# Adding the mask to a quarter of the bias tiles on GpSimd, with stacks loaded in halves and a new table of slots

## Chip, cores and metric

The kernel runs on one core of a Trainium2 chip. The metric is device time in microseconds, the median over executions; a change below about 0.2% (2 us here) can't be told from none.

## What is computed

Sixteen sequences of 256 x 256 (float32) go through four layers. Layer 0 is a gradient and Laplacian step. Layer 1 is an adapter (down, gelu, a chosen expert, up, layer norm). Layer 2 is two modulated silu projections with norms over the whole matrix. Layer 3 is an attention block with 16 heads of 16 features and a feed-forward part of 1024. The change is in the attention:

```
scores = einsum('bhqd,bhkd->bhqk', q / sqrt(16), k)
scores = scores + attention_bias
scores = where(src_mask, -inf, scores)
probs = softmax(scores)
```

The bias is a tensor of 16 x 16 x 256 x 256; the mask is shared by the heads of a sequence. The kernel takes -1e30 for minus infinity and adds it.

## The kernel before

The work goes by **pairs** of sequences, eight of them, and a pair has 32 heads (16 for each sequence b = 0, 1). The function `run` writes out the order of every engine: a turn per pair has 32 **slots**, and slot n holds head n of pair j, steps of the `back` (what follows the attention) of the pairs j, j-1 and j-2, and steps of the `front` (layers 0 to 2 and q, k, v) of pair j+1 and the end of pair j's own. The table `AT` (with `AT_FIRST` for pair 0 and `AT_LAST` for the last) says in which slot each step of b = 0 and b = 1 stands; a slot of 32 or more is that slot less 32 of the next turn. Every engine walks the same slots in program order, at its own pace, and waits on semaphores. All 32 slots of pair 0's front come before the first head; after the last head only the back of the last pair is left.

A head goes through the engines like this:
- SyncE (`turn` at L462) loads the bias of heads in chunks of two into a ring of four buffers. A chunk waits until ScalarE is done with the chunk four before it (`prob_ok`). The same queue carries `load_stacks`, at positions given by `SP_AT`.
- TensorE (`scores`, L1321): a product of the identity with `mask_add` (bf16, 128 x 512, L1325) puts the mask of the head into PSUM; two products of the stacks (96 rows, bf16, L1328) add q times k. The stacks hold q and k split into bf16 parts; they are written to DRAM (L1006) and read back as six transfers for each sequence (L448).
- VectorE (`bias_and_max`, L893): L901 adds the PSUM scores and the bias tile and takes the row maximum, twice for each head.
- ScalarE: exp (L1038), and two heads later the copy of the turned probabilities (L1051). TensorE turns them (L1342) and multiplies four heads at once by V (L1363).

GpSimd runs what is left: two products of layer 0 (L554), additions of bias rows (L566, L575, L607), the scale and shift `x4` (L586, L588), the conversion of the mask (L536), and `inv_std` (L541), the power -1/2 that norms wait for. Those with 128 x 512 elements have eight forms (L554 has two), and each comes twice in a pair.

Steps that the prediction names: `hn` is the normalising of the attention output by VectorE (L646 with `ffT` as output), which waits for `inv5` on GpSimd; `ctx_spread` (L597) is a GpSimd copy that waits for the end of a group of heads on VectorE.

The four lines that put the mask in:

```python
pe.matmul(SP_[:, h % 2, :], identb[:, :], mask_add[:, 2 * b:2 * b + 2, :].rearrange("p q k -> p (q k)"),
          start=True, stop=False)
...
                    stacks[1][:, b, hh, :], start=False, stop=(q == 1))
```

Of the kernel before, what the change touches and what calls it, by code (L numbers as in the profile page):

```python
# [16 lines left out]
ALU = mybir.AluOpType  # L17
# [23 lines left out]
CH = 2  # L41
# [28 lines left out]
AT = {"x4": (21, 43), "ctx_spread": (16, 41), "ctx": (20, 36), "ctx_scale": (20, 36), "wo": (21, 37), "x5": (21, 38),  # L70
# [3 lines left out]
      "store": (46, 52), "prods_p": (1, 14), "prods": (1, 13), "diffs": (2, 15), "edges": (3, 15), "l0": (4, 17),  # L74
# [6 lines left out]
      "q_split": (25, 40), "q_out": (25, 42), "k": (25, 40), "kf": (25, 40), "k_split": (26, 41), "k_out": (26, 41),  # L81
      "v": (28, 45), "V": (29, 47), "mask": (20, 2)}
AT_FIRST = {"s_trig": (1, 1), "s_onehot": (2, 2), "s_grid": (1, 1), "s_h1": (1, 1), "s_h2": (5, 5), "s_h2t": (6, 6),
            "s_sel": (2, 2), "s_cond": (10, 10), "s_condt": (11, 11), "s_mask": (23, 23), "s_rows": (16, 16),
# [19 lines left out]
GROUPS = HEADS // GROUP  # L104
BATCHES = HEADS // BATCH


ORDER = [0, 2, 4, 6, 1, 3, 5, 7]
PR = 2
SIG = 1.702  # L110
WARM = {"begin": 50, ("w_in", 0): 8}


def wait_alone(eng, sem, value):


# [1341 lines left out]
```

## Time and profile before

| | |
|---|---|
| median of 3 runs | 993.87 us (991.92 to 994.06) |
| the profiled execution | 994.1 us, its span 992.3 us |
| TensorE matmul busy | 878.8 us, 89% of the span |
| VectorE busy | 767.2 us, 77% |
| ScalarE busy | 733.7 us, 74% |
| GpSimd busy | 238.5 us, 24% |
| first scores product | 102.1 us from the start |
| last head's scores | 958.5 us |

Six pairs in the middle repeat each other every 110.9 us. Busy time of TensorE is modelled: a matmul's record is longer than the distance to the next one (378 ns against 216 ns for 128 x 256 in float32), so the distance between starts is what one costs. Some records of L1325 are missing (168 of 256 matmuls, while the 256 weight loads are all there).

### The profile page before, as it was taken

The page shows a single profiled execution, that of the slowest core. Times are in us where ns is not written, and L with a number is a line of the kernel's source. Part 1 is how long each engine was busy: PE and PEld are TensorE (multiplying, and loading weights), DVE is VectorE, ACT ScalarE, POOL GpSimd, SP SyncE. Part 2 cuts the span into 40 slices and gives each one's busy share as a digit, 9 for nine tenths or more (in the row PEclk, how much of TensorE's full clock was granted, in tenths as well). Part 3 has the DMA queues.
Part 4 walks back from the last instruction along what each step waited for, and adds up shares of the span by engine and source line. Part 5 has one row for each costly group of instructions (what it writes and reads, how often), then busy time and mean ns, then how long its engine had stood idle before and what let it go on. Part 6 is the DMA issues. An engine that isn't in the chain of part 4 may idle for free.

```text
span 992.3 us, 17959 instructions
## 1 busy us (share of the span) xinstructions
PE 878.8 (89%) x5643; PEld 663.2 (67%) x5731; DVE 767.2 (77%) x2375; ACT 733.7 (74%) x1901; POOL 238.5 (24%) x237
## 2 busy tenths in 40 slices
PE   6775678998999989998999989998999989999988
PEld 5454455776777767776777767776777767766666
DVE  7366678978887988978887888888887988866532
ACT  2123578988788787978888787978789787978672
POOL 2124122312242222312242222312242223111100
PEclk8677789999999999999999999999999999999999
DMA  9714464463737364563628364553637273555500
GB/s 255 223 44 90 133 155 128 128 165 96 164 103 191 102 134 125 137 154 107 170 95 189 97 153 123 127 146 111 167 107 191 81 169 108 124 142 141 165 15 22
DMA packets 128472, 130.86 MB, mean 132 GB/s; under 512 B 16729, under 2 KB 121945, under 8 KB 125289
## 3 DMA queue, kind: packets, MB, share of 16 engines
q1 hardware_dynamic: 96464, 111.49, 43.5%
q10 hardware_dynamic: 31914, 18.23, 6.5%
q8 instruction: 46, 0.75, 0.3%
q14 instruction: 48, 0.39, 0.1%
HBM read 112.61 MB, written 17.07 MB: 131 GB/s over the span
## 4 chain that ended last, share of the span: by engine, by line
PE 54%; DVE 18%; ACT 16%; issue 7%; DMA 3%; POOL 1%; SPq 0%; DVEq 0%; ACTq 0%; POOLq 0%
PE ff_ps L1316 9%; PE PT_ps L1342 8%; PE ctx_ps L1363 5%; PE G L1112 5%; ACT Pr L1038 5%; PE scores_ps L1328 4%; PE ff_ps L1297 4%; DVE bias L901 3%; ACT L1038 3%; PE G L1197 3%; PE G L1120 3%; ACT PT L1051 2%; PE scores_ps L1325 2%; PE ff_ps L1283 2%; PE G L1193 2%
## 5 line engine op out<-in xcount | busy, mean ns | idle before, releaser
L1038 ACT ACTIVATE Pr<-bias,nmax 128x256 f32<-128x256 f32 x512 | 255.7, 502 | 135.2 <-DVE nmax L901 110.1
L901 DVE CUSTOM_DVE_ANT_0 bias<-scores_ps,bias 128x256 f32<-128x256 f32 x512 | 195.9, 420 | 85.8 <-issue 45.5
L1342 PE MATMUL PT_ps<-ident,Pr 128*128 128x128 f32 x1024 | 159.2, 278 | 9.4 <-ACT PT L1051 9.4
L1051 ACT ACTIVATE PT<-PT_ps 128x512 f32<-128x512 f32 x256 | 148.3, 579 | 0.2 <-PE PT_ps L1342 0.2
L1342 PEld LDWEIGHTS PT_ps<-ident,Pr 128*128 128x128 f32 x1024 | 117.3, 141 | 42.2 <-issue 27.1
L541 POOL TENSOR_TENSOR rstd<-var,half_neg 128x2 f32<-128x2 f32 (+1 forms) x64 | 40.4, 632 | 402.2 <-DVE var L666 233.3
L1297 PE MATMUL ff_ps<-ctxT,w 128*128 128x256 f32 x480 | 116.0, 384 | 7.1 <-ACT ffT L1025 6.3
L1316 PE MATMUL ff_ps<-w,ffT 128*128 128x256 f32 x480 | 112.3, 380 | 0.0
L1328 PE MATMUL scores_ps<-k_stack,q_stack 96*128 96x256 bf16 x512 | 99.9, 276 | 10.0 <-DMA k_stack<-part_dram 4.1
L1297 PEld LDWEIGHTS ff_ps<-ctxT,w 128*128 128x128 f32 x480 | 86.4, 190 | 20.6 <-ACT ffT L1025 10.3
L1038 ACT ACTIVATION_READ_ACCUMULATOR Pr<-bias,nmax 128x1 f32 x512 | 97.6, 191 | 0.0
L1316 PEld LDWEIGHTS ff_ps<-w,ffT 128*128 128x128 f32 x480 | 87.2, 190 | 10.2 <-issue 0.4
L1363 PE MATMUL ctx_ps<-PT,V 128*32 128x256 f32 x1024 | 68.8, 386 | 17.3 <-ACT PT L1051 17.3
L1328 PEld LDWEIGHTS scores_ps<-k_stack,q_stack 96*128 96x128 bf16 x512 | 51.0, 100 | 48.1 <-issue 2.5
L1325 PE MATMUL scores_ps<-mask_add,identb 128*128 128x512 bf16 x168 | 64.9, 387 | 1.1 <-issue 1.0
L1038 ACT ACT_TABLE_LOAD x44 | 56.5, 1283 | 5.4 <-DVE nmax L901 4.7
L880 DVE SCALAR_TENSOR_TENSOR ffT<-tanh,ffT 128x512 f32<-128x512 f32 x60 | 44.3, 738 | 18.7 <-ACT ffT L1025 18.7
L1363 PEld LDWEIGHTS ctx_ps<-PT,V 128*32 128x32 f32 x1024 | 28.0, 109 | 42.6 <-issue 20.5
L987 ACT ACT_TABLE_LOAD x31 | 39.8, 1283 | 17.5 <-DVE cond L743 13.5
L1021 ACT ACTIVATE tanh<-ff_ps,b1s 128x256 f32<-128x256 f32 x120 | 50.0, 471 | 3.0 <-PE ff_ps L1297 3.0
L1025 ACT ACTIVATE ffT<-ff_ps,b 128x256 f32<-128x256 f32 x120 | 50.8, 485 | 0.0
L597 POOL COPY tanh<-rinv 128x512 f32<-128x512 f32 x16 | 9.8, 610 | 146.9 <-DVE ctxU L913 146.9
(219 smaller groups left out, 1693.5 us busy)
## 6 DMA issues: line engine op xcount, KB each, us to landing
bias<-in_fside_Bx16xSxS_dram SPq DMA_DIRECT2D x256, 256.0 KB, 3.1
part_dram<-front ACTq DMA_DIRECT2D x32, 384.0 KB, 2.7
q_stack<-part_dram SPq DMA_DIRECT2D x16, 384.0 KB, 4.8
k_stack<-part_dram SPq DMA_DIRECT2D x16, 384.0 KB, 7.9
F<-in_x_dram SPq DMA_DIRECT2D x16, 256.0 KB, 3.8
ada<-rows_dram SPq DMA_DIRECT2D x16, 256.0 KB, 5.6
q_stack<-part_dram SPq DMA_DIRECT2D x16, 256.0 KB, 5.6
k_stack<-part_dram SPq DMA_DIRECT2D x16, 256.0 KB, 8.7
```

Source lines behind the costliest of these rows:

```text
L901: nc.vector.tensor_tensor_reduce(out=t, in0=SP_[:, n % 2, q * S:(q + 1) * S], in1=t, scale=-1.0, scalar=BIG, op0=ALU.add, op1=ALU.min, acc ...
L1021: nc.scalar.activation(tanh_at(j, b, m)[:, e * S:(e + 1) * S], bank("w1", j, b, m)[:, e, :], ACT.Tanh, bias=b1s[:, f:f + 1], scale=SIG / 2)
L1025: ins = nc.scalar.activation(ff_at(j, b)[:, f, :], bank("w1", j, b, m)[:, e, :], ACT.Identity, bias=b1[:, f:f + 1])
L1038: ins = nc.scalar.activation(Pr[:, n % PR, q, :], bias[:, n // CH % RING, 2 * (n % CH) + q, :], ACT.Exp, bias=nmax[:, n, q:q + 1], scale=-1.0,
L1051: nc.scalar.activation(PT[:, m % BATCH, :, :].rearrange("p c q -> p (c q)"), TP[:, m % 2, :], ACT.Identity).then_inc(pt_ok, 1)
L1112: ins = pe.matmul(GF[b][:, m, :], w[:, c, m * P:(m + 1) * P], xT[:, c, :], start=(c == 0), stop=(c == 1))
L1297: ins = pe.matmul(bank("w1", j, b, m)[:, e, :], w1[:, c, f * P:(f + 1) * P], ctxT[:, c, b * S:(b + 1) * S], start=(c == 0), stop=(c == 1))
L1316: ins = pe.matmul(Ft[:, t, :], ffT[:, f, t * P:(t + 1) * P], w2[:, f, :], start=(f == 0), stop=(f == FB - 1))
L1325: pe.matmul(SP_[:, h % 2, :], identb[:, :], mask_add[:, 2 * b:2 * b + 2, :].rearrange("p q k -> p (q k)"), start=True, stop=False)
L1328: ins = pe.matmul(SP_[:, h % 2, q * S:(q + 1) * S], stacks[0][:, b, hh, q * P:(q + 1) * P], stacks[1][:, b, hh, :], start=False, stop=(q = ...
L1342: ins = pe.transpose(TP[:, m % 2, c * S + q * P:c * S + (q + 1) * P], Pr[:, m % PR, q, c * P:(c + 1) * P], ident[:, :])
L1363: ins = pe.matmul(CP[n * TILE:(n + 1) * TILE, 0:S], V[:, 2 * b + c, half * BATCH + n, odd * DH:odd * DH + TILE], PT[:, n, c, :], start=(od ...
```

## The change

GpSimd adds `mask_add` to the bias tiles of the heads in slots 3 and 7 of each eight, three slots ahead. VectorE waits for `bias_masked` at these heads in place of `bias_loaded`, and TensorE leaves out the mask product for them (64 of 256). Each stack is loaded in two halves of eight heads, with its own semaphore. The slots are laid anew. Of the tables, only lines that the text speaks of are shown.

```diff
@@ slots
...
-AT = {"x4": (21, 43), "ctx_spread": (16, 41), "ctx": (20, 36), "ctx_scale": (20, 36), "wo": (21, 37), "x5": (21, 38),
-      "inv5": (21, 43), "hn": (22, 39), "hn_turn": (24, 40), "hT": (23, 40), "x5b": (38, 49),
...
-      "aff0": (12, 28), "x2b": (13, 27), "y0": (12, 28), "w_in": (13, 29), "z": (14, 31), "avg1": (16, 32),
-      "var1": (16, 32), "inv2": (15, 38), "aff1": (17, 33), "y1": (17, 33), "w_out": (19, 35), "x3": (19, 36),
...
+AT = {"x4": (28, 42), "ctx_spread": (16, 35), "ctx": (20, 37), "ctx_scale": (20, 36), "wo": (21, 37), "x5": (21, 38),
+      "inv5": (24, 42), "hn": (21, 39), "hn_turn": (23, 40), "hT": (22, 40), "x5b": (29, 51),
...
+      "aff0": (12, 28), "x2b": (13, 30), "y0": (12, 28), "w_in": (13, 29), "z": (14, 31), "avg1": (16, 33),
+      "var1": (15, 33), "inv2": (15, 34), "aff1": (17, 34), "y1": (17, 33), "w_out": (19, 35), "x3": (19, 35),
...
-AT_FIRST = {... "s_mask": (23, 23), ... "x2b": (4, 28), ... "inv1": (9, 27), ...}
+AT_FIRST = {... "s_mask": (29, 29), ... "x2b": (10, 26), ... "inv1": (14, 25), ...}
-SP_AT = {"front": (0, 7), "stacks": (1, 9), "mask": 6, "rows": (12, 3)}
+SP_AT = {"front": (0, 7), "stacks": (1, 2, 9, 11), "mask": 6, "rows": (12, 3)}
+MASKED_EARLY = (3, 7)
+MASK_AHEAD = 3
@@ SyncE
+            def load_stacks(j, b, g):
+                mine = slice(g * GROUP, (g + 1) * GROUP)
+                if g == 0:
+                    wait_alone(sp, part_written[b], (j + 1) * 32)
...
+                        src = part_in[w, b, order[s] * DH:(order[s] + count) * DH, mine]
+                        sp.dma_start(stacks[w][s * DH:(s + count) * DH, b, mine, :], src
+                                     ).then_inc(stack_loaded[2 * b + g], 16)
...
+                        for g in range(2):
+                            if c == SP_AT["stacks"][2 * b + g]:
+                                if not first:
+                                    wait_alone(sp, score_mm, (j - 1) * HEADS + b * H + (g + 1) * GROUP)
+                                load_stacks(j, b, g)
@@ GpSimd
+            def add_mask(j, n):
+                if n % GROUP not in MASKED_EARLY:
+                    return
+                c, b = n // CH, n // H
+                pool.wait_ge(mask_ok, 2 * j + b + 1)
+                pool.wait_ge(bias_loaded[c % RING], (j * (NCH // RING) + c // RING + 1) * 16 * CH)
+                mine = bias[:, c % RING, 2 * (n % CH):2 * (n % CH) + 2, :]
+                nc.gpsimd.tensor_tensor(mine, mine, mask_add[:, 2 * b:2 * b + 2, :], ALU.add).then_inc(bias_masked, 1)
             def head(j, n, with_back):
+                if j == 0 and n == 0:
+                    for m in range(MASK_AHEAD):
+                        add_mask(0, m)
+                if n < HEADS:
+                    turns, m = divmod(n + MASK_AHEAD, HEADS)
+                    if j + turns < PAIRS:
+                        add_mask(j + turns, m)
@@ VectorE
-                dve.wait_ge(bias_loaded[c % RING], (j * (NCH // RING) + c // RING + 1) * 16 * CH)
+                if n % GROUP in MASKED_EARLY:
+                    dve.wait_ge(bias_masked, masked_by(j, n))
+                else:
+                    dve.wait_ge(bias_loaded[c % RING], (j * (NCH // RING) + c // RING + 1) * 16 * CH)
@@ TensorE
-                pe.matmul(SP_[:, h % 2, :], identb[:, :], mask_add[...], start=True, stop=False)
+                early = h % GROUP in MASKED_EARLY
+                if not early:
+                    pe.matmul(SP_[:, h % 2, :], identb[:, :], mask_add[...], start=True, stop=False)
...
-                                    stacks[1][:, b, hh, :], start=False, stop=(q == 1))
+                                    stacks[1][:, b, hh, :], start=early, stop=early or q == 1)
-                    pe.wait_ge(stack_loaded[n // H], (j + 1) * 16 * 2 * len(STACK_RUNS))
+                if n < HEADS and n % GROUP == 0:
+                    pe.wait_ge(stack_loaded[n // GROUP], (j + 1) * 16 * 2 * len(STACK_RUNS))
```

## Rows read from the trace of the kernel before

**Rows 1.** The page: busy time of each engine, and the chain by engine.

```profile
PE 878.8 (89%) x5643; PEld 663.2 (67%) x5731; DVE 767.2 (77%) x2375; ACT 733.7 (74%) x1901; POOL 238.5 (24%) x237
...
PE 54%; DVE 18%; ACT 16%; issue 7%; DMA 3%; POOL 1%; SPq 0%; DVEq 0%; ACTq 0%; POOLq 0%
```

**Rows 2.** Windows: pair 3, length, then busy PE, PEld, DVE, ACT, POOL; clock, DMA.

```profile
429.03:539.96 110.93, 103.06 (x680) 78.63 (x691) 94.13 (x291) 91.12 (x238) 29.62 (x29) 1.00 0.51 134
```

**Rows 3.** The chain that ended last, pair 3: start, length, what.

```profile
438.62 0.22 PE scores_ps L1325
...
451.26 0.22 PE scores_ps L1325
...
468.58 0.70 DVE front L799
...
483.14 0.38 PE scores_ps L1328 x2
...
496.28 0.22 PE scores_ps L1325
...
509.61 1.28 ACT L1038
...
523.52 0.21 PE scores_ps L1325
...
537.52 0.22 PE scores_ps L1325
```

**Rows 4.** Timeline around one head's scores, TensorE matmuls: start, length, line.

```profile
485.52 0.38 PE L1325 MATMUL scores_ps<-mask_add,identb 128*128 128x512 bf16 x1
...
485.74 0.39 PE L1328 MATMUL scores_ps<-k_stack,q_stack 96*128 96x256 bf16 x2
...
485.96 0.60 PE L1342 MATMUL PT_ps<-ident,Pr 128*128 128x128 f32 x4
```

**Rows 5.** Groups by line in pair 3: count, busy us, mean ns, idle before.

```profile
L646 DVE TENSOR_SCALAR ffT<-x,back_mv,back_rstd 128x256 f32<-128x256 f32 x4 | 5.4, 1386 | 0.1
...
L646 DVE TENSOR_SCALAR front<-front,mv,rstd 128x256 f32<-128x256 f32 x8 | 2.9, 408 | 0.1
...
L756 DVE TENSOR_TENSOR front<-F,gB 128x512 f32<-128x512 f32 x2 | 2.4, 1218 | 0.0
...
L756 DVE TENSOR_TENSOR front<-F,gU 128x512 f32<-128x512 f32 x2 | 1.4, 681 | 0.0
```

**Rows 6.** Timeline, VectorE and GpSimd at two places of pair 3.

```profile
508.94 1.27 POOL L586 TENSOR_TENSOR x<-front,ada 128x512 f32<-128x512 f32 x1
...
509.01 2.70 DVE L646 TENSOR_SCALAR ffT<-x,back_mv,back_rstd 128x256 f32<-128x256 f32 x2
...
510.29 1.27 POOL L588 TENSOR_TENSOR x<-x,ada 128x512 f32<-128x512 f32 x1
...
529.78 1.71 POOL L554 TENSOR_TENSOR front<-F,gB 128x512 f32<-128x512 f32 x1
...
530.56 0.43 DVE L901 CUSTOM_DVE_ANT_0 bias<-scores_ps,bias 128x256 f32<-128x256 f32 x1 [0.19 <-PE scores_ps L1328]
```

**Rows 7.** The chain that ended last, before the first head.

```profile
87.69 2.75 DMA part_dram<-front
...
93.92 8.00 DMA k_stack<-part_dram
...
102.54 0.63 PE scores_ps L1328 x2
```

**Rows 8.** Timeline of GpSimd before the first head.

```profile
74.97 3.06 POOL L536 TENSOR_SCALAR mask_add<-mask_raw 128x512 bf16<-128x512 uint8 x2
...
90.72 1.27 POOL L575 TENSOR_TENSOR front<-front,b_out 128x512 f32<-128x512 f32 x1
```

**Rows 9.** The page, DMA issues: count, KB each, median us to landing.

```profile
bias<-in_fside_Bx16xSxS_dram SPq DMA_DIRECT2D x256, 256.0 KB, 3.1
```

**Rows 10.** Timeline of SyncE's queue: bias loads of four heads of pair 3.

```profile
419.73 5.52 SPq L474 DMA_DIRECT2D bias<-in_fside_Bx16xSxS_dram  x4
```

More of the change, by code:

```diff
@@ L69 @@
 SLOTS = HEADS
-AT = {"x4": (21, 43), "ctx_spread": (16, 41), "ctx": (20, 36), "ctx_scale": (20, 36), "wo": (21, 37), "x5": (21, 38),
[3 rows of a table removed]
-      "store": (46, 52), "prods_p": (1, 14), "prods": (1, 13), "diffs": (2, 15), "edges": (3, 15), "l0": (4, 17),
[6 rows of a table removed]
[L81 to L84, printed above, removed]
-            "x4": (30, 44), "s_fill": (0, 0), "s_bq": (17, 17), "s_w2": (24, 24), "prods_p": (0, 12),
-            "prods": (1, 11), "diffs": (1, 13), "edges": (3, 14), "l0": (2, 18), "x1": (3, 21), "relu": (5, 16),
[6 rows of a table removed]
-            "q_split": (25, 40), "q_out": (24, 41), "k": (23, 40), "kf": (24, 40), "k_split": (26, 41),
-            "k_out": (24, 41), "v": (24, 45), "V": (29, 45)}
@@ L95 @@
-AT_LAST = {"ctx_spread": (15, 40), "ctx": (20, 36), "ctx_scale": (20, 38), "wo": (21, 36), "x5": (21, 39),
[3 rows of a table removed]
-           "store": (78, 89)}
-SP_AT = {"front": (0, 7), "stacks": (1, 9), "mask": 6, "rows": (12, 3)}
+AT = {"x4": (28, 42), "ctx_spread": (16, 35), "ctx": (20, 37), "ctx_scale": (20, 36), "wo": (21, 37), "x5": (21, 38),
[3 rows of a table added]
+      "store": (51, 51), "prods_p": (0, 14), "prods": (2, 13), "diffs": (2, 15), "edges": (2, 15), "l0": (4, 17),
[6 rows of a table added]
+      "q_split": (25, 40), "q_out": (26, 41), "k": (25, 40), "kf": (25, 40), "k_split": (26, 41), "k_out": (26, 42),
+      "v": (28, 45), "V": (29, 45), "mask": (20, 2)}
@@ new lines @@
+AT_FIRST = {"s_trig": (0, 0), "s_onehot": (0, 0), "s_grid": (0, 0), "s_h1": (0, 0), "s_h2": (4, 4), "s_h2t": (8, 8),
+            "s_sel": (1, 1), "s_cond": (9, 9), "s_condt": (12, 12), "s_mask": (29, 29), "s_rows": (16, 16),
+            "x4": (30, 40), "s_fill": (5, 5), "s_bq": (7, 7), "s_w2": (28, 28), "prods_p": (3, 13), "prods": (2, 3),
+            "diffs": (2, 16), "edges": (2, 17), "l0": (1, 17), "x1": (3, 18), "relu": (5, 18), "x1_turn": (1, 18),
+            "x1T": (5, 18), "res1": (3, 24), "down": (5, 19), "hid": (5, 19), "expert": (5, 19), "expT": (6, 19),
[7 rows of a table added]
@@ L101 @@
+AT_LAST = {"ctx_spread": (22, 33), "ctx": (20, 40), "ctx_scale": (20, 37), "wo": (21, 40), "x5": (21, 38),
[3 rows of a table added]
+           "store": (61, 70)}
+SP_AT = {"front": (0, 7), "stacks": (1, 2, 9, 11), "mask": 6, "rows": (12, 3)}
 END = 2 * SLOTS
@@ L286, in adapter_to_attention_kernel @@
         bias_loaded = [sem(f"bias_loaded{n}") for n in range(RING)]
+        bias_masked = sem("bias_masked")
         prods = sem("prods")
@@ L303, in adapter_to_attention_kernel @@
         part_written = [sem(f"part_written{b}") for b in range(2)]
-        stack_loaded = [sem(f"stack_loaded{b}") for b in range(2)]
+        stack_loaded = [sem(f"stack_loaded{n}") for n in range(4)]
         mask_ok, identb_ok = sem("mask_ok"), sem("identb_ok")
@@ L408, in head_at, with masked_by @@
             return b, slot // GROUP * GROUP + ORDER[slot % GROUP]
+        def masked_by(j, n):
+            return sum(m % GROUP in MASKED_EARLY for m in range(j * HEADS + n + 1))
         def lagged(j, n, lag, with_back):
@@ L456, in turn @@
                             load_front(j + 1, b)
-                        if c == SP_AT["stacks"][b]:
-                            if not first:
-                                wait_alone(sp, score_mm, (j - 1) * HEADS + (b + 1) * H)
-                            load_stacks(j, b)
+                        for g in range(2):
[3 more added lines that the diff above has]
+                                load_stacks(j, b, g)
                     if c == SP_AT["rows"][1]:
@@ L1324, in scores @@
                 pe.wait_ge(biased, LEAD + j * 2 * HEADS + 2 * max(h - 1, 0))
-                pe.matmul(SP_[:, h % 2, :], identb[:, :], mask_add[:, 2 * b:2 * b + 2, :].rearrange("p q k -> p (q k)"),
-                          start=True, stop=False)
+                early = h % GROUP in MASKED_EARLY
+                if not early:
+                    pe.matmul(SP_[:, h % 2, :], identb[:, :], mask_add[:, 2 * b:2 * b + 2, :].rearrange("p q k -> p (q k)"),
+                              start=True, stop=False)
                 for q in range(2):
```

5 lines of the change are left out of this document (removed), and 31 rows, old and new, of tables (AT, AT_FIRST, AT_LAST).

## The prediction

> **What bounds the kernel now.** I read the page first. TensorE is the busiest engine with 89% of the span, but that is an average over a start, eight pairs and an end, and VectorE (77%) and ScalarE (74%) are not far off [rows 1]. So I went to one pair out of the six that repeat. There TensorE is busy 103.1 of 110.9 us at the full clock, VectorE 94.1, ScalarE 91.1 and GpSimd only 29.6 [rows 2]. TensorE is the bound, and the other two have 17 and 20 us to spare. The third view is the chain that ended last in this pair. It is mostly TensorE, but it leaves TensorE for VectorE and ScalarE in some stretches. That matters here, since a TensorE product that is removed while the chain is elsewhere gives nothing. I found the heads by counting the 32 groups of scores from 429.0. The heads in question are 3, 7, 11, 15, 19, 23, 27 and 31. Six of them are on the chain: 3, 7, 19, 27 and 31 with their mask product, and 15 at 483.14, where the record of the mask product is missing but the scores are in the chain. Head 11 falls in the stretch around 468.58 in which the chain is on VectorE, and head 23 beside the one at 509.61 in which it is on ScalarE [rows 3].
>
> **The mask products.** A record of L1325 says 0.38 us, but the next matmul starts 0.22 us after it, and the pair of L1328 takes 0.22 us more until the transposes start [rows 4]. The weight load hides below the matmul before. So a removed product is worth 0.22 us of TensorE, and nothing has to be put in its place. All 64: 64 x 0.22 = 14 us, the upper end. Six of eight on the chain: 6 x 0.22 = 1.3 us a pair, 8 pairs, 10.5 us. The lower end is 0, if the other chains are as long. I take 10.5 us, because the rows show where the heads stand.
>
> **The additions on GpSimd.** There are 64 of them, 128 x 512, one float32 operand and one bf16. The trace has none with a bf16 operand; the nearest row is the operations of the same size in float32, 1.27 us [rows 6]. The operand types leave room both ways; the mask conversion, 1.53 us apiece (3.06 for two), is the other end [rows 8]. Eight of them are 10.2 us a pair (12.2 at that end), so GpSimd goes from 29.6 to some 40 of 110 us, still by far the least busy. By itself this costs nothing. Two things on it can cost.
>
> First, waiting. VectorE at head n now needs GpSimd to be through with everything that stands ahead of slot n-3. GpSimd waits longest at `ctx_spread` (slot 16), which needs VectorE's slot 19; the next addition (head 23) stands behind it, with four heads, some 13 us, to spare. The bias must have landed before the addition: it takes 3.1 us [rows 9], and the loads that are issued from 419.7 on are those of heads 2 to 5, while the scores of head 3 stand at 438.6 [rows 10, 3]. So the bias is there some 15 us before, and the addition has its 1.3 us. Queued behind an addition are `inv0` to `inv3` and `inv5`, 0.6 to 0.7 us each, which VectorE waits for; an addition in front of one delays it by at most 1.3 us. Price: 0 as a rule; I keep 0.3 us a pair in mind for the upper end.
>
> Second, the two engines get in each other's way. At 508.94 the two operations of `x4` run on GpSimd, and the two L646 of `hn` beside them take 2.70 us, where the same operation elsewhere takes 0.41 [rows 6, 5]. L901, which has one operand in PSUM, is not slowed: 0.43 us in the middle of an L554 that runs to 531.5 [rows 6]. The groups give the price per pair: L646 of `hn` (1386 - 408) x 4 = 3.9 us, L756 with gB (1218 - 681) x 2 = 1.1 us, together 5.0 us for 16 long operations of GpSimd (eight forms, two of each), 0.31 us each [rows 5]. Eight additions make 2.5 us more of VectorE in a pair. VectorE has 17 us to spare, and the chain is on it for 18% of the time [rows 1]. So 2.5 x 0.2 = 0.5 us a pair reach the end, 4 us in all. The ends: nothing, or all of it, 8 x 2.5 = 20 us.
>
> The Trainium skill (page "SBUF — State Buffer", section "Who interferes with whom") states a rule that speaks against this change: a VectorE instruction with two SBUF inputs, or in a 2-port mode, and a GpSimd instruction that reads SBUF hold a port pair exclusively, and the second one blocks fully until the first is done. The two L646 that end with the two `x4` operations agree with it, and so does L901. By that rule alone each addition could cost VectorE its whole length, 64 x 1.27 = 81 us of VectorE time; the sum above goes by the mean of the rows instead, since most VectorE work at a given moment is not of the kind that is held.
>
> **The stacks in halves.** Head 0 of pair 0 waits for all of b = 0's stacks: the parts are written from 87.7 to 90.4, the six loads are issued up to 93.9, the last lands 8.0 us later, and the scores start at 102.5 [rows 7]. With halves the same number of issues brings half of the bytes, so the last landing should take about 4 us; head 0 starts 4 us earlier. Ends: 8.0 - 2.75 = 5.2 us, if a half lands as fast as one written part [rows 7], and 0, if something else holds head 0. The candidate is the mask: its conversion goes from slot 23 to slot 29, behind `inv1` and `x2b` of b = 1. `x2b` ends at 92.0 and the conversions take 3.1 [rows 8], so the mask is ready at some 95, ahead of the half stack at 98. In the other pairs I put nothing for the halves. I take 4 us. The twelve more issues a pair are on SyncE's queue, which waits for buffers most of the time; cost 0, and at most their 0.4 us each in front of bias loads that have 15 us to spare.
>
> **The slots.** Most steps move by one or two slots. One move answers to a row: `inv5` and `x4` of b = 0 stood both in slot 21, so `x4` ran right beside `hn` [rows 6]. Now they are in 24 and 28, which saves VectorE about 2.70 - 0.82 = 1.9 us a pair. The chain is on ScalarE there (509.61) [rows 3], so little of it reaches the end. b = 1 keeps both in slot 42 and keeps its collision. `hn` in slot 21 now waits for an `inv5` behind the addition for head 27; that bias has the same 15 us of lead over its head, six heads further on, so it should be there a little before `hn` asks, and I put no wait. The removed waits and new ones I can't add up: I take -0.3 us a pair, -2.5 us in all, between -10 and +12 us.
>
> **Sum**, against the profiled execution's own 994.1 us: -10.5 -4 +4 -2.5 = -13, that is 981.1. The median of the runs is 993.9, 0.2 lower. Forecast: 981.
>
> **The rivals.**
> 1. *The gain is taken up by waits.* TensorE has 7.9 us of idle time a pair [rows 2], and each place where it waits for VectorE or ScalarE can swallow what was saved before. For it: the chain is off TensorE in good parts of a pair, head 23 among them [rows 3]. Against it: six of eight products are on it. Then only the start's 4 us are left: 990, between 985 and 995. Chance 0.20.
> 2. *More than forecast.* All eight products count, the collision at `hn` counts and the new slots save 1 us a pair: -14 -4 -8 +2 = -24, that is 970. Chance 0.14.
> 3. *Slower: the additions hold VectorE.* If each addition meets an operation that it holds up, as `x4` does with `hn` (0.98 us for each L646 [rows 5]), VectorE gets 8 us more a pair and is at 102 of 111, as busy as TensorE at 103.1 - 1.7 = 101.4. If half of it passes on, 4 - 1.3 = 2.7 us a pair are lost, 21 us in all, less the start's 4: 1011. It decides as soon as more than 1.8 us a pair reach the end (1.3 of the products and 0.5 of the start). Against it: L901 and all PSUM readers are not touched. Chance 0.14.
>
> **The chances.** The forecast has 0.52. Faster by over 0.2%: all of the forecast and of rival 2 and most of rival 1 (0.12), 0.78. Within: 0.08, from rivals 1 and 3. Slower: 0.14. The range from 966 to 998 takes in the forecast, rival 1 and most of rival 2, and the lower part of rival 3, and leaves out about 0.2. 0.2% is about what a measurement of this kernel can tell from no change.
>
> **What would show it.** Right: 192 weight loads of L1325, a period of about 109.3 us, head 0 at 98, GpSimd additions of 1.3 us, VectorE some 1 us busier or the same in a pair (2.5 more, 1.9 less), and waits for `bias_masked` that don't show. A period of 110.9 with more idle time of TensorE is rival 1. VectorE's busy time over 98 us a pair, with L646, L756 or L880 drawn out beside the additions, is rival 3. Wrong in a way I have not priced: VectorE idle ahead of L901 until the addition ends.

## The result, and the profile after

The change makes the kernel slower. Its median is 1001.0 us (998.3 to 1002.1, five runs), against 991.9 us (989.8 to 994.1) for the kernel before on the same chip: the ratio is 1.0087, with a 95% interval from 1.0066 to 1.0108. The forecast was 981 us. The profiled execution took 1002.1 us, 8.0 us more than that of before. One execution of e5 below (4795 us) and one of e6 (2176 us) were in a slow state and are left out of their medians.

The change shifts line numbers: L931 is L901 of before, L673 is L646, L1360 is L1328, L1374 is L1342, L551 is L541, L1068 is L1038. The additions are L627, `out` is L914, `ctx_scale` L889, `ctx_spread` L607. In columns of the granted clock 1.00 is TensorE's 2.4 GHz and 0.50 its 1.2 GHz.

The page of the changed kernel: busy time of each engine, the chain by engine, the group of the additions, and four DMA issues.

```profile
PE 870.7 (87%) x5590; PEld 661.5 (66%) x5667; DVE 763.6 (76%) x2375; ACT 732.8 (73%) x1901; POOL 316.0 (32%) x301
...
PE 47%; ACT 22%; DVE 21%; issue 8%; POOL 2%; DMA 1%; DVEq 0%; ACTq 0%; POOLq 0%
...
L627 POOL TENSOR_TENSOR bias<-bias,mask_add 128x512 f32<-128x512 f32 x64 | 76.8, 1200 | 80.6 <-DMA bias<-in_fside_Bx16xSxS_dram 80.5
...
q_stack<-part_dram SPq DMA_DIRECT2D x32, 192.0 KB, 3.4
k_stack<-part_dram SPq DMA_DIRECT2D x32, 192.0 KB, 3.9
```

TensorE has 8 us less work and the span grew all the same. The chain moved [rows 1]: TensorE's part fell from 54% to 47%, VectorE's and ScalarE's rose from 34% to 43% together. Time taken from TensorE is time that the chain now spends elsewhere. In the third row the last number is the one to stop at: GpSimd stood idle for 80.5 us until a bias tile had landed.

A cut of the two profiled executions into stretches, by the first product of scores of each pair, says where the 8 us are:

| stretch | before | after | difference |
|---|---|---|---|
| start to head 0 of pair 0 | 102.2 | 97.7 | -4.5 |
| pair 0 | 105.0 | 105.0 | 0 |
| pairs 1 to 6, each | 110.9 | 112.5 | +1.56 (six: +9.4) |
| pair 7 to the last head's L931 (L901 before) | 86.4 | 86.0 | -0.4 |
| from there to the end | 33.1 | 36.7 | +3.6 |

So three things are to be explained: the start, which came out near the forecast; the pair, which should have lost 1.6 us and gained as much; and the end, on which the forecast had no term.

The windows of pair 4 of the changed kernel, in the columns of [rows 2].

```profile
540.40:653.00 112.60, 102.44 (x674) 78.21 (x683) 93.70 (x292) 90.84 (x237) 38.21 (x36) 1.00 0.47 129
```

TensorE is idle for 10.2 us of this pair, where it was 7.9 before (in both, some records of the mask product are missing, and a little of the idle time is theirs). VectorE is no busier than before (94.1), so rival 3 doesn't stand in this row. What makes up VectorE's 93.7 stands in two groups of the same pair.

```profile
L673 DVE TENSOR_SCALAR front<-front,mv,rstd 128x256 f32<-128x256 f32 x8 | 5.2, 687 | 0.0
L673 DVE TENSOR_SCALAR ffT<-x,back_mv,back_rstd 128x256 f32<-128x256 f32 x4 | 3.4, 899 | 0.9 <-POOL back_rstd L551 0.8
```

Beside [rows 5]: `hn` went from 1386 to 899 ns (1.9 us saved by the four, the collision of b = 0 is gone), and the normalising of the front (L673 with `front`) from 408 to 687 ns (2.2 us lost by the eight). In e10 below, which has the same table and no additions, it takes 471 ns, so 1.7 of the 2.2 us are the additions'. Both sizes are near those of the prediction. They are busy time, though, not time on the path.

The timeline shows what happens between the heads. First VectorE and ScalarE in slot 2 of pair 4.

```profile
546.88 0.69 DVE L783 TENSOR_TENSOR front<-F,gB 128x512 f32<-128x512 f32 x1
...
552.42 0.25 DVE L801 TENSOR_REDUCE front<-edge_p 128x4 f32<-128x16 f32 x2
552.59 0.24 DVE L942 RECIPROCAL rinv<-rsum 128x16 f32<-128x16 f32 x1
552.75 0.36 DVE L943 COPY ctxU<-ctx_ps 128x256 f32<-128x256 f32 x1
553.02 0.41 DVE L931 CUSTOM_DVE_ANT_0 bias<-scores_ps,bias 128x256 f32<-128x256 f32 x1
...
553.53 0.51 ACT L1068 ACTIVATE Pr<-bias,nmax 128x256 f32<-128x256 f32 x1 [2.56 <-PE PT_ps L1374]
```

The new table puts `prods`, `diffs` and `edges` of b = 0 all in slot 2. VectorE works 5.8 us on them in one piece (546.88 to 552.67), and only then does L931 of head 3, whose scores TensorE had begun at 546.5. ScalarE stands idle for 2.56 us. (The row names the transposes, which ended at 553.46, since they came last; but by the program this exp waits for the transposes of head 1, of 546.80, and for head 3's first maximum, which was ready at 553.44.)

It is the most striking stall of the pair, and yet the chain that ended last does not go through it:

```profile
547.40 3.46 PE ff_ps L1346 x16
550.86 1.73 PE G L1150 x8
552.64 0.38 PE scores_ps L1360 x2
...
559.41 1.53 DVE front L673 x2
```

From 545.09 to 558.01 the chain is on TensorE with no other piece than 0.05 us of issue, and TensorE has work all that time: the last pieces of `w2` (L1346), which the new table puts in slot 35, that is slot 3 of the next turn, and `w_out` (L1150). It leaves TensorE at 558.04, for VectorE, and comes back for good at 568.52, by way of ScalarE, GpSimd and VectorE. Here are GpSimd, VectorE and TensorE in that stretch.

```profile
559.33 1.60 DVE L673 TENSOR_SCALAR front<-front,mv,rstd 128x256 f32<-128x256 f32 x2
559.63 1.16 POOL L627 TENSOR_TENSOR bias<-bias,mask_add 128x512 f32<-128x512 f32 x1 [1.40 <-DMA bias<-in_fside_Bx16xSxS_dram]
...
565.71 1.27 POOL L596 TENSOR_TENSOR x<-front,ada 128x512 f32<-128x512 f32 x1
565.77 2.69 DVE L673 TENSOR_SCALAR ffT<-x,back_mv,back_rstd 128x256 f32<-128x256 f32 x2
...
568.52 0.66 PE L1130 MATMUL ff_ps<-ident,ffT 128*128 128x128 f32 x4 [1.15 <-DVE ffT L673]
```

An addition starts when its bias lands, by chance beside `xn3`, and draws it out to 1.60 us. Of the 0.78 us that this adds, TensorE's next matmul (L1130, at 560.99) waits 0.21. The lower three rows are the collision of `x4` with `hn` that the new table keeps for b = 1; TensorE waits 1.15 us for it, and it waited 0.91 us at the same place before. The first of the two is new, the second is not.

### The profile page after: what moved, and what is told of

The parts are those of the page before. It is cut to its first block, busy times and chain, and to the rows that moved or that the text cites. A ratio compares the mean times of both kernels' runs of the same rounds, so it can differ in the third digit from the quotient of the medians.

```text
span 1000.3 us, 18087 instructions
## 1 busy us (share of the span) xinstructions
PE 870.7 (87%) x5590; PEld 661.5 (66%) x5667; DVE 763.6 (76%) x2375; ACT 732.8 (73%) x1901; POOL 316.0 (32%) x301
## 4 chain that ended last, share of the span: by engine, by line
PE 47%; ACT 22%; DVE 21%; issue 8%; POOL 2%; DMA 1%; DVEq 0%; ACTq 0%; POOLq 0%
PE ff_ps L1346 9%; ACT Pr L1068 7%; PE PT_ps L1374 7%; PE ctx_ps L1395 5%; DVE bias L931 4%; PE G L1227 4%; ACT PT L1081 3%; PE ff_ps L1327 3%; PE scores_ps L1360 3%; ACT L1068 3%; PE G L1142 3%; PE G L1150 3%; DVE front L673 2%; DVE ffT L673 2%; ACT L1017 2%
## 5 line engine op out<-in xcount | busy, mean ns | idle before, releaser
L1068 ACT ACTIVATE Pr<-bias,nmax 128x256 f32<-128x256 f32 x512 | 255.8, 502 | 142.4 <-DVE nmax L931 115.2
L931 DVE CUSTOM_DVE_ANT_0 bias<-scores_ps,bias 128x256 f32<-128x256 f32 x512 | 194.3, 420 | 70.8 <-issue 42.5
L551 POOL TENSOR_TENSOR rstd<-var,half_neg 128x2 f32<-128x2 f32 (+1 forms) x64 | 40.3, 629 | 388.0 <-DVE var L693 256.3
L1374 PE MATMUL PT_ps<-ident,Pr 128*128 128x128 f32 x1024 | 159.1, 278 | 3.7 <-ACT PT L1081 2.8
L1374 PEld LDWEIGHTS PT_ps<-ident,Pr 128*128 128x128 f32 x1024 | 117.5, 141 | 35.2 <-issue 28.6
L1346 PE MATMUL ff_ps<-w,ffT 128*128 128x256 f32 x480 | 112.9, 381 | 0.6 <-DVE ffT L907 0.6
L1360 PE MATMUL scores_ps<-k_stack,q_stack 96*128 96x256 bf16 x512 | 99.5, 275 | 4.3
L627 POOL TENSOR_TENSOR bias<-bias,mask_add 128x512 f32<-128x512 f32 x64 | 76.8, 1200 | 80.6 <-DMA bias<-in_fside_Bx16xSxS_dram 80.5
L1068 ACT ACTIVATION_READ_ACCUMULATOR Pr<-bias,nmax 128x1 f32 x512 | 97.6, 191 | 0.0
L1346 PEld LDWEIGHTS ff_ps<-w,ffT 128*128 128x128 f32 x480 | 87.1, 190 | 11.3 <-DVE ffT L907 1.0
L1360 PEld LDWEIGHTS scores_ps<-k_stack,q_stack 96*128 96x128 bf16 x512 | 50.4, 100 | 40.4 <-issue 3.3
L1357 PE MATMUL scores_ps<-mask_add,identb 128*128 128x512 bf16 x115 | 44.6, 388 | 0.7 <-DVE nmax L931 0.7
```

The costliest lines, as they stand in the source:

```text
L627: nc.gpsimd.tensor_tensor(mine, mine, mask_add[:, 2 * b:2 * b + 2, :], ALU.add).then_inc(bias_masked, 1)
L931: nc.vector.tensor_tensor_reduce(out=t, in0=SP_[:, n % 2, q * S:(q + 1) * S], in1=t, scale=-1.0, scalar=BIG, op0=ALU.add, op1=ALU.min, acc ...
L1068: ins = nc.scalar.activation(Pr[:, n % PR, q, :], bias[:, n // CH % RING, 2 * (n % CH) + q, :], ACT.Exp, bias=nmax[:, n, q:q + 1], scale=-1.0,
L1346: ins = pe.matmul(Ft[:, t, :], ffT[:, f, t * P:(t + 1) * P], w2[:, f, :], start=(f == 0), stop=(f == FB - 1))
L1360: ins = pe.matmul(SP_[:, h % 2, q * S:(q + 1) * S], stacks[0][:, b, hh, q * P:(q + 1) * P], stacks[1][:, b, hh, :], start=early, stop=earl ...
L1374: ins = pe.transpose(TP[:, m % 2, c * S + q * P:c * S + (q + 1) * P], Pr[:, m % PR, q, c * P:(c + 1) * P], ident[:, :])
```

## The experiments

Fifteen kernels ran, four to twelve executions each. Each is made from the changed kernel by putting parts of it back, or from another of the fifteen; "old slots" means the three tables of before, "whole stacks" the loads of before. The ratio is always to the kernel before, on the same chip. Where it and a difference of two medians disagree, the ratio counts. The period is the mean over pairs 1 to 6 of the one profiled execution, and "end" the time from the last head's L931 on. With whole stacks the lines after the loads are numbered three lower.

### The parts alone: additions, slots, halves

```diff
-MASKED_EARLY = (3, 7)        # e2, e3
+MASKED_EARLY = ()
-AT, AT_FIRST, AT_LAST of after   # e1, e3, e4
+AT, AT_FIRST, AT_LAST of before
-"stacks": (1, 2, 9, 11)      # e1, e2, with load_stacks and its waits as before
+"stacks": (1, 9)
```

> Slots and whole stacks of before; only the additions on GpSimd in place of 64 mask products. Theory A (the new slots cost the time): the products give most of what the prediction's sum has for them, 0.5 to 1.3 us a pair less than 110.9, 4 to 10 us faster than before. Theory B (the additions hold VectorE or its queue): the period is 112 us or more and the kernel 8 us or more slower than before.

> The new slots alone, with all 256 mask products on TensorE and whole stacks. Theory A: the slots alone make the loss, period 112.5 us or more, 12 to 20 us slower than before, with an end that is 3 us longer. Theory B: the slots cost nothing by themselves, within 3 us of before.

> Slots of before, no additions, stacks in halves. Both theories: head 0 of pair 0 starts 4 to 5 us earlier (98 in place of 102.5) and all of it stays to the end: 4 to 6 us faster than before. If the head start is lost later, the same as before.

> The whole change except for the slots, which are those of before. Theory A: 8 to 15 us faster than before, 978 to 985. Theory B: slower than before by 3 us or more, since the start's 4.5 us don't make up for the additions.

| kernel | additions | slots | stacks | median | ratio (95%) | period | end |
|---|---|---|---|---|---|---|---|
| e1 | yes | old | whole | 1102.9 | 1.1139 (1.1108 to 1.1170) | 126.5 | 33.4 |
| e2 | no | new | whole | 1002.9 | 1.0118 (1.0094 to 1.0142) | 112.2 | 36.5 |
| e3 | no | old | halves | 987.0 | 0.9958 (0.9943 to 0.9972) | 111.0 | 33.1 |
| e4 | yes | old | halves | 1087.9 | 1.0972 (1.0942 to 1.1002) | 124.5 | 33.4 |
| change | yes | new | halves | 1001.0 | 1.0087 (1.0066 to 1.0108) | 112.5 | 36.7 |

Halves alone give 4.2 us, as forecast. Where they give it is not as forecast: head 0 of e3 starts at 99.9 us and not at 98, 2.3 us earlier than before, and another 3.4 us are saved inside pair 0. The last load of the half lands at 97.7 there, so head 0 no longer waits for it, but for the front of b = 1. The new slots alone cost 12 us, just under the 12 to 20 of theory A, where the prediction took a gain of 2.5. And with the additions in the old slots e1 is 113 us slower than before: theory B of e1 (a loss of 8 us and more) holds, by far more than it had in mind. The table of waits of e1 names the mechanism (who waited for what: sum in us, times, longest; L604 is `ctx_spread` there).

```profile
POOL bias L624 <- DMA bias<-in_fside_Bx16xSxS_dram: 229.2, 31, 14.2
...
PE ff_ps L1301 <- POOL tanh L604: 47.6, 7, 7.8
```

The chain of e1 shows one such case from end to end.

```profile
584.72 8.90 DMA bias<-in_fside_Bx16xSxS_dram
...
594.87 2.50 POOL front L561 x2
...
599.03 1.15 POOL bias L624
600.18 1.24 POOL x L614
601.42 0.55 POOL rstd L548
```

The load of the bias went out behind the six loads of a whole stack and took 8.9 us. GpSimd takes its instructions in order, as the rows show, so L561, L614 and `inv_std` (L548), on which VectorE waits in turn, stood behind an addition that waited for it. The addition does not use the time of GpSimd that was counted as free; it holds the queue. TensorE waits 5.9 to 7.8 us for `ctx_spread` in each of seven pairs, and in each of the six in the middle its clock is at 1.2 GHz for at least 13.7 us around that place. The new slots of the change are therefore no bonus beside the additions. They are what the additions have to be paid with, and with halves they bring the loss from 96 us (e4) down to 9.

### Which of the old slots the additions break

```diff
-"ctx_spread": (16, 41) ... "inv2": (15, 38) ... "inv3": (18, 41)
+"ctx_spread": (16, 35) ... "inv2": (15, 34) ... "inv3": (18, 38)    # e5, e6, e7, e11: old slots and halves
-"x5b": (38, 49)
+"x5b": (29, 49)                                                     # e11 only
```

e6 leaves the mask out at the 64 heads altogether (no product and no addition, and VectorE waits for `bias_loaded` at all heads again, so its output is another); e7 keeps the products beside the additions, so the mask is added twice there.

> Mask on GpSimd and halves with the old slots, except that three GpSimd steps of b = 1 stand earlier: ctx_spread 35 in place of 41, inv3 38 in place of 41, inv2 34 in place of 38. Theory Q (the 100 us of e1 and e4 come from these steps standing behind an addition whose bias load waits for ScalarE): they go away with these three moves alone, and the kernel is under 1000. If also the products give what the prediction has (1.3 us a pair) and the port little: 977 to 983. If the additions take back what the products give: 985 to 990, about the 987.0 of the halves alone. If theory Q is wrong: over 1050.

> As e5, but at the heads of slots 3 and 7 of each eight the mask is left out altogether: no product and no addition. It prices the products alone. By the prediction 10 us faster than the halves alone (987.0), 975 to 979. If the waits take up the gain: 985 to 988.

> As e5, but the products stay as well, so the mask is added twice at these heads. It prices the additions alone. By the prediction 4 us slower than the halves alone: 989 to 993, with 2.5 us more of VectorE a pair. If each addition holds up an operation of VectorE on the path: 1000 or more.

> As e5, with x5b of b = 0 in slot 29 in place of 38, so that it no longer stands behind the addition for head 7. Theory: the rest of e5's loss is this one wait (1.9 us of TensorE, after which its clock is at half for some 8 us). Then the period falls from 114 to 117 us to between 110 and 111.5 and the kernel to 982 to 992. If the additions themselves hold VectorE: over 1000.

Measured: e5 1025.1 us, 1.0330 (1.0304 to 1.0357); e6 988.0, 0.9960 (0.9945 to 0.9975); e7 1030.0, 1.0381 (1.0361 to 1.0402); e11 1013.3, 1.0231 (1.0211 to 1.0251), with a period of 112.5. Three moves take 64 us off e4 (by the ratios), so these steps were the larger part of the loss; but theory Q had the kernel under 1000, and it isn't. Between e5 and e6 stands what the additions still cost, 37 us. e7 is 5 us slower than e5: beside the additions, too, the 64 products are worth no more than that. e6 is at 988, the upper of its two theories: the removed products and the three moves come out even against e3 (e9, below, has the products' gain without the moves). A part of the 37 us is one place in each pair, here in the timeline of e5.

```profile
569.39 1.16 POOL L627 TENSOR_TENSOR bias<-bias,mask_add 128x512 f32<-128x512 f32 x1
570.51 1.26 POOL L617 TENSOR_TENSOR x<-x,b 128x512 f32<-128x512 f32 x1
...
571.87 0.69 DVE L914 TENSOR_TENSOR x<-ff_ps,x 128x512 f32<-128x512 f32 x1 [2.53 <-POOL x L617]
...
572.62 0.66 PE L1304 MATMUL ff_ps<-ident,tanh 128*128 128x128 f32 x4 [1.85 <-DVE x L914]
```

One addition of 1.16 us in front of `x5b` (L617) is most of the 1.85 us that TensorE waits. What followed it in pair 4 stands in the windows of e5 around it (length, TensorE's busy time, granted clock; the last two columns are the DMA's share and rate).

```profile
568.00:573.00 5.00, 3.15 (x20) 1.00 0.32 96
573.00:581.00 8.00, 8.00 (x29) 0.57 0.10 24
581.00:590.00 9.00, 7.87 (x61) 1.00 0.36 110
```

After a stretch in which TensorE was busy for 3.15 of 5.0 us the mean granted clock of the next 8 us was 0.57, so most of them passed at 1.2 GHz. Eight us at 0.57 hold the work of 4.6 at 2.4 GHz: the place costs up to 3.4 us beyond the wait. But the wait alone doesn't bring the clock down. All six pairs of e5 have it, of 1.84 to 1.86 us each. In pairs 1, 4 and 5 the clock was at 1.2 GHz for 6.8 us from 0.4 to 1.4 us behind its end on, and they took 117.5, 117.0 and 117.5 us; in pairs 2 and 6 it stayed at 2.4 GHz, and they took 112.9 and 113.7. (Pair 3 had 3.4 us at 1.2 GHz, some 23 us later, and took 114.1.) So about 4 us of such a pair hang on the clock, and whether they are paid changes from pair to pair. The waits of e1 and e4 are longer, 5.7 to 7.8 us, and the clock fell at every one; e1's mean clock is 0.922, that of before 0.965.

e11 moves `x5b` out of the way, and its period falls from 115.5 to 112.5. Its theory had 110 to 111.5 and 982 to 992 us, and over 1000 if the additions themselves hold VectorE; it is at 1013. Against e9 (below), which has neither additions nor products at the 64 heads, it lost 16 us in pair 0, whose own table was not moved. The trace has it there: GpSimd waits 5.63, 3.95 and 11.91 us for bias tiles, and TensorE 7.95 us for L1017 of ScalarE and 5.61 us for L684 of VectorE, where no wait of TensorE in e9's pair 0 is over 1.6 us. That points at the held queue once more. e4, e5 and e7 have the same long pair 0 (115 to 119 us against e9's 101.5).

### What a product is worth, and an addition

```diff
                 if n % GROUP not in MASKED_EARLY:
                     return
+                return        # e9: old slots and halves, neither product nor addition at the 64 heads
```

> The halves alone (e3), and at the heads of slots 3 and 7 of each eight the mask left out altogether, with no step moved. If the products stand on the chain as the prediction counted them: 1.3 us a pair, 977 against 987. If the waits behind them take up the gain: less than half of it, a period over 110.2 us and 982 or more.

> The changed kernel without its additions: new slots, halves, all 256 products on TensorE. It tells what additions and products together are worth in the new slots. If they come out even: 998 to 1001, a period of 112.2. If the additions cost more than the products give: 994 to 997.

VectorE's wait for `bias_masked` is taken out of e9 as well. e9 (mask left out at 64 heads) took 980.4 us, 0.9893 (0.9880 to 0.9906), e10 (the change without additions, all 256 products) 997.6, 1.0065 (1.0051 to 1.0080). Both are between their two theories: e9 gives more than half of the forecast gain and not all of it, and e10 is 0.4 us below the range for "they come out even". The windows of pair 4, in this order: e3, e9, e11, e10; the change's own stands above.

```profile
535.00:646.00 111.00, 103.79 (x692) 78.63 (x691) 94.09 (x291) 91.08 (x238) 29.70 (x29) 1.00 0.48 133
```

```profile
530.30:640.40 110.10, 102.30 (x683) 77.91 (x682) 93.91 (x291) 91.05 (x237) 29.67 (x29) 1.00 0.49 137
```

```profile
555.20:667.90 112.70, 102.87 (x683) 77.94 (x682) 99.14 (x291) 91.41 (x237) 39.31 (x37) 1.00 0.48 130
```

```profile
535.00:647.20 112.20, 104.09 (x691) 78.87 (x690) 91.25 (x291) 90.94 (x238) 29.70 (x28) 1.00 0.47 133
```

- *Products.* e3 and e9 differ by the products alone: 0.0065 in the ratio (6.5 us) and 0.96 us in the period (0.83 without pair 2 of e3, in which the clock fell for 3.4 us). In the old slots eight removed products are worth 0.8 to 1.0 us a pair, not 1.3: TensorE's busy time falls by 1.5 us and its idle time rises by 0.6.
- *Additions, VectorE's time.* e9 to e11 adds 5.2 us of VectorE in a pair (99.14 less 93.91), 0.65 us for each addition; e10 to the change adds 2.45 (93.70 less 91.25), 0.31 for each. The prediction took 0.31 from the rows. That is right in the new slots, and half of it in the others: the price is where the addition falls.
- *Additions, the path.* e11's period is 2.4 us above e9's. Up to 1.4 us of it may be the moved steps (e6 has 111.45 where e9 has 110.09), so the additions cost 1.0 to 2.4 us a pair there, as much as the products give or more, and the 16 us of pair 0 come on top. In the new slots products and additions together come to +0.2 us a pair (112.26 to 112.50), and the ratios differ by 0.0022 (+2.2 us), with intervals that overlap. TensorE's busy time falls by 1.65 us (104.09 to 102.44) and its idle time rises by 2.1 (8.1 to 10.2; nine records of mask products are missing in the latter, so both are somewhat less). Its waits of over 0.3 us grow from 7.6 to 8.9 us a pair. Here waits take up the whole gain.

By the Trainium skill (page "SBUF — State Buffer", section "Who interferes with whom"), when a VectorE instruction that uses the port pair shared with GpSimd meets one of GpSimd, the one issued first has the pair for its whole length and the other is blocked. The trace agrees where two of them meet (559.33, above): the first L673 of the two takes its usual 0.41 us, and the second, which starts at 559.65 behind the addition of 559.63, takes 1.28 us and ends 0.14 us after it. But the full 1.16 us for each addition are not in the sums: 0.31 and 0.65.

### The new slots taken apart

```diff
-AT_LAST of after
+AT_LAST of before                             # e8: the change, old table for the last pair
-"ctx": (20, 37), "w2": ((31, 33, 35, 35), ...)
+"ctx": (20, 36), "w2": ((31, 33, 33, 34), ...)  # e12: the change, these two put back
-"prods_p": (1, 14), "prods": (1, 13), "edges": (3, 15)
+"prods_p": (0, 14), "prods": (2, 13), "edges": (2, 15)  # e13: e3 with these; e15: e10 with them put back
```

e14 is e3 with `ctx`, `w2`, `hn`, `hn_turn`, `hT`, `w1` and `h1` where the change has them. Of the theories on record e8's first holds for the end; e12 and e14 came out slower than either of theirs; e13 is just past its theory A, and e15 is in its theory B.

> The changed kernel with the old table for the last pair alone. If the table of the last pair makes the longer end (36.6 us behind the last head's maximum in place of 33.1): 3 to 4 us faster than the changed kernel, 997 to 998, with an end of 33 us. If the end is longer for the additions: the same 1001.

> The changed kernel with two steps of TensorE put back: ctx of b = 1 from slot 37 to 36, and w2 of b = 0 from 31, 33, 35, 35 to 31, 33, 33, 34. If these two make most of what the new slots lose in a pair (0.9 us of waiting for ctxT ahead of wo, 0.5 us ahead of the first product by V): a period of 111.2 us in place of 112.5, and 10 us faster than the changed kernel, 989 to 993. If it is the VectorE steps of slot 2: no change, 1001.

> The old slots with halves and all 256 mask products, no additions (987.0 us, period 110.95 us), with one thing of the new table: the three VectorE steps of layer 0 for b = 0 stand where the change put them (prods_p in slot 0, prods and edges in slot 2 behind each other with diffs). Theory A: these cost the new slots their 1.3 us a pair, since VectorE is held 5 us in slot 2 and ScalarE waits for head 3: period 112 to 112.5 and 995 to 999 us. Theory B: the cost comes of the moved steps of the back (ctx, w2, hn) or of the norms: period within 0.3 us of 110.95 and 985 to 989 us.

> The old slots with halves and all products, no additions, with seven moves of the new table in the back: ctx of b = 1 from 36 to 37, w2 of b = 0 to (31, 33, 35, 35), hn, hn_turn and hT of b = 0 a slot earlier, and w1 and h1 with them. Theory A (the cost is in the steps of slot 2): period within 0.3 us of 110.95, 985 to 989 us. Theory B (it is in the back): period over 111.6, 992 to 999 us. hn a slot earlier should still be held by x4, since x4 stays in slot 21 here.

> The new table with halves and all products, no additions (997.6 us, period 112.3 us), with the three VectorE steps of layer 0 for b = 0 put back in slots 1, 1 and 3. Theory A: period 111.0 to 111.4, some 989 us. Theory B: the moved steps belong together and putting three back gives nothing or costs: 996 us or more.

| kernel | made from | median | ratio (95%) | period | end |
|---|---|---|---|---|---|
| e8 | change | 999.2 | 1.0064 (1.0040 to 1.0088) | 112.5 | 33.4 |
| e12 | change | 1026.8 | 1.0363 (1.0343 to 1.0384) | 116.7 | 35.0 |
| e13 | e3 | 999.3 | 1.0067 (1.0051 to 1.0084) | 113.2 | 33.2 |
| e14 | e3 | 1028.6 | 1.0369 (1.0349 to 1.0388) | 117.2 | 33.2 |
| e15 | e10 | 1029.2 | 1.0379 (1.0361 to 1.0398) | 117.7 | 34.8 |

*The end.* With the old `AT_LAST` the stretch after the last head is back at 33.4 us from 36.7. The ratios differ by 0.0023, with intervals that overlap: the end of the profile is shown, its share of the median is not. Only half of the 3.6 us is the table itself. e10, e12 and e15 have the new `AT_LAST` and an end of 34.8 to 35.0 us. In the change and in e2 (36.7 and 36.5) the clock falls to 1.2 GHz for 3.4 us in the middle of the end (981.9 to 985.4 in the change), which is worth 1.7 us. Before pair 7 the two kernels are the same, and still pair 0 took 111.8 us in the profiled execution of e8 and 105.0 in that of the change. The granted clock is one difference: 1.2 GHz from 112.2 to 119.1 in e8, 2.4 GHz from 111.5 on in the change. That is worth up to 3.4 us, and the rest is open. The start of this kernel varies from one execution to the next by more than most terms here; a reader who takes a few us from one profile at the start is misled.

*The pair.* The three VectorE steps of layer 0 alone, in an otherwise old table, cost 10.8 us (e3 to e13, by the ratios). The timeline of e13, slot 2 of pair 4:

```profile
548.34 0.58 ACT L1081 ACTIVATE PT<-PT_ps 128x512 f32<-128x512 f32 x1
552.83 0.51 ACT L1068 ACTIVATE Pr<-bias,nmax 128x256 f32<-128x256 f32 x1 [3.92 <-DVE nmax L931]
```

It is the stall of the changed kernel, only longer: ScalarE waits 3.92 us while VectorE is busy with the three steps. And here TensorE waits too, 1.59 us at 553.74, for L914 (`out`), which stands behind L931 on VectorE. Head 5's scores come 1.8 us later in the pair than in e3. So in the old table theory A holds.

In the new table it isn't shown. e15 puts the three back and gets 5.5 us a pair worse; e12 puts two steps of the back back and gets 4 us worse. TensorE's timelines of the two show one and the same place, between heads 4 and 5 of pair 4 (e12, then e15), and the windows of e12 behind it (columns as above).

```profile
568.73 0.66 PE L1304 MATMUL ff_ps<-ident,tanh 128*128 128x128 f32 x4 [2.69 <-DVE x L914]
```

```profile
567.89 0.39 PE L1219 MATMUL G<-zeros 1*128 1x512 bf16 x1 [2.11 <-DVE front L801]
```

```profile
565.40:570.80 5.40, 2.70 (x18) 1.00 0.08 24
570.80:574.20 3.40, 3.40 (x9) 0.50 0.53 160
```

TensorE waits there in each of the six pairs, 2.7 us in e12 and 2.1 in e15, and in each of them the clock falls there, to 1.2 GHz for 3.4 or 6.8 us, which is worth 1.7 or 3.4 us. Together that is about what the two kernels lose. In the changed kernel and in e10 TensorE doesn't wait there, and the clock stays at 2.4 GHz through the six pairs. I read this as moves that belong together: `w2` in slot 35 gives TensorE its 3.46 us of L1346 while VectorE is held by the three steps of slot 2. With one of the two put back, TensorE stands still, and the clock falls.

What is left, the 1.2 us a pair from e3 to e10, is 1.0 us of idle time of TensorE in other places: a second wait for `ctxT` (L889) ahead of `wo` (L1313), 0.79 us, at head 5; 0.98 us for L1017 of ScalarE at head 29; 0.4 us more ahead of the products by V; less two waits of the old table that are gone (0.73 and 0.43 us). Which moves make them was not tested.

The seven moves of the back alone, in the old table, lose 6.1 us a pair (e14). Its timeline shows a part of it, at head 5 of pair 4.

```profile
574.45 0.69 DVE L889 TENSOR_TENSOR ctxT<-ff_ps,ctxU 128x512 f32<-128x512 f32 x1 [4.10 <-PE ff_ps L1304]
...
577.58 0.51 ACT L1068 ACTIVATE Pr<-bias,nmax 128x256 f32<-128x256 f32 x1 [5.92 <-DVE nmax L931]
```

`ctx` stands in slot 37 for TensorE, and `ctx_scale`, its reader on VectorE, is still in slot 36, in front of head 5. VectorE waits 4.1 us for a product that TensorE has queued a head later, and ScalarE 5.9 us behind it. In the changed kernel, where VectorE comes late out of slot 2, the same wait at L889 is 0.95 us. One delay is hidden behind another: the table can't be judged step by step, and no single move was found that explains the 1.2 us.

## Why the prediction was wrong

Point by point, with the terms of its sum:

- **The stacks in halves: right in size.** 4 us taken, 4.2 us by the ratio of e3; the 4.5 us of the profile are one execution's, and the start varies (head 0 stands at 92.9 us in e10, which has the slots and halves of the change, and at 100.1 in e2, which has its slots and whole stacks). The load of a half stack took 3.4 to 3.9 us, as reckoned. Head 0 of e3 came 2.3 us earlier and not 4, as said above. In the changed kernel head 0 no longer waits for the stacks, but for eight products of `w_in`, which stand ahead of it on TensorE and run from 94.1.
- **The products: the right reason, too large.** 10.5 us taken, 6.5 measured in the old slots (e3 to e9). The count of six in eight on the chain was near (1.0 us of 1.7 is between four and five), but the chain of one execution is not the chain after the change. In the new table TensorE waits for others at the places where products went, and the change from e10, +0.2 us a pair, says that nothing of them is left once the additions are paid.
- **The additions, waiting: the step that failed on its mechanism.** It read "So the bias is there some 15 us before" from loads issued at 419.7 and scores at 438.6 [rows 10, 3], less the median of 3.1 us [rows 9]. These four loads stand right behind six of a stack, and the same trace has their own landing time (issues of 419.5 to 425.4, median us):

```profile
bias<-in_fside_Bx16xSxS_dram SPq DMA_DIRECT2D x4, 256.0 KB, 8.1
```

The bias of head 3 landed at 429.6, 8.8 us before its scores. That is the shortest lead among the eight heads of the pair (the longest is 25.3), and it counts from the wrong place: the addition stands three slots ahead, where TensorE was at 429.0, and an idle GpSimd asks earlier still. GpSimd waited 80.5 us for bias tiles in 30 waits in the changed kernel, 229 us in e1. The price of 0 rested on this step. And the prediction priced one addition in front of a step by its own 1.3 us, not by the wait that the addition itself may have. Of the 100 us from e3 to e4, three moves of steps that stood behind an addition give back 64 (e5). In the new slots the price of the waiting was not measured by itself.
- **The additions, the port: right in size, wrong in weight.** 2.5 us of VectorE a pair were forecast and 2.45 measured. The 0.5 us a pair that were to reach the end rest on the share of the chain (18%), which is no rate of passing on: what counts is who waits for the instruction that is drawn out. How much of it passes was not measured by itself. At the one place looked at, 0.21 of 0.78 us of `xn3` reached TensorE.
- **The slots: the largest error.** "I take -0.3 us a pair, -2.5 us in all, between -10 and +12 us." Measured: +1.07% or +10.6 us from e3 to e10, and +1.18% or +11.7 us from before to e2, the upper end. The range said it, the sum did not. The prediction followed one move for its 1.9 us (which came, in busy time) and didn't follow the others, some of which cost much by themselves: three steps of layer 0 in slot 2 (10.8 us in e13), seven moves of the back (e14, 41 us). Together in the new table, with the rest, they cost 10.6 us, no more than the first alone. The slack of 17 to 20 us of VectorE and ScalarE is a mean over a pair and was nil in slot 2. Which waits of TensorE make the loss is measured, which moves make the waits is open.
- **The sum of what was measured,** by the ratios, 0.01 being 9.9 us: halves -4.2 (before to e3), new slots +10.6 (e3 to e10), products and additions together +2.2 (e10 to the change), in all +8.6. If the products gave in the new slots the 6.5 us that they give in the old ones, the additions would cost some 9 us; they weren't taken apart there.

Of the rivals the first came nearest in kind: the gain of the products is taken up by waits (busy time down by 1.65 us, idle time up by 2.1, from e10 to the change). But it stopped at 990, since it had no new wait in it and no cost of the slots. Rival 3 gave 1011 for a slower kernel by a VectorE that is held; its sign came true, its mechanism is in the trace and is not what decides: VectorE is at 93.7, not at 102. The mistake in the price of -2.5 us for the table was to put a small number on what it "can't add up by hand".

The halves alone (e3), at 0.9958 (0.9943 to 0.9972), are the best of the kernels that compute the whole, and beat both.

## What to carry to other kernels

Work given to an idle engine costs its queue, not only its time: ask for each new instruction what it waits for, how late that can be at the worst place, and who stands behind it. Take the landing time of the very loads it waits for, not the median of all. When a change comes with a new order of the steps, price the order as a part of its own; run it alone if you can, since its moves may cover one another and can't be added up. A long stall of an engine off the chain need not cost anything, so look first whether the busiest engine has work meanwhile. Slack summed over a pair says nothing about a slot.

## What the runs showed of the hardware

- A wait of TensorE of 1.85 us, in a stretch where it was busy for 3.15 of 5.0 us, was followed by 8 us at a mean granted clock of 0.57 (e5, pair 4), so that wait and clock together cost up to 5.3 us. The same wait in pairs 2 and 6 of e5 was not followed by a lower clock. Waits of 2.1 us (e15) and 2.7 us (e12) came with 3.4 or 6.8 us at 1.2 GHz in each of the pairs 1 to 6.
- Two VectorE operations of 128 x 256 (L673) of which the second met a GpSimd addition took 0.41 and 1.28 us; the second ended 0.14 us after the addition.
- The GpSimd addition of 128 x 512 with a bf16 operand took 1.16 us at best and 1.20 on the average, less than the 1.27 us of the all-float32 form [rows 6].
- A bias load that was issued right behind six loads of a whole stack took 8.9 us to land (e1), and four of them in before took 8.1 us in the median; over the whole kernel the median is 3.1 us, before and after.
- The same instruction stream took 105.0 and 111.8 us for pair 0 in two profiled executions (the change and e8), with the clock at 1.2 GHz for 6.9 us in one at a place where the other had 2.4 GHz.
